# Strassen products on eight cores: an old layer's last M6 and M7 go between M2 and M1 of the new layer, token sums follow need, W3's blocks load on another queue

## What is computed

```python
xn = _layernorm(x)                      # x: 8192 x 2048, float32
xz = einsum('bsh,ih->bsi', xn, W_in)    # 2048 -> 2 x 4096
x1, z = split(xz, 2)
x1 = einsum('bsk,ik->bsi', x1, conv_w)  # 4096 -> 4096
a = einsum('bsi,hi->bsh', (x1 * D) * silu(z), W_out)    # 4096 -> 2048
h = relu(xn @ W1.T + b1); h = relu(h @ W2.T + b2)       # 2048 -> 4096 -> 4096
out = x + a + (h @ W3.T + b3)                           # 4096 -> 2048
```

## Time and profile before

| | us |
|---|---|
| median of 3 runs | 1953.33 |
| lowest, highest | 1846.08, 2122.7 |
| the profiled execution | 1847.9 |
| its span on the slowest core (core 5) | 1846.4 |
| spans of the eight cores | 1838.6 to 1846.4 |

### The profile page before, as it was taken

One profiled execution on the slowest core, in us unless ns is written; L12 is line 12 of the kernel. 1 busy time (PEld: TensorE's weight loads), 2 busy tenths in 40 slices (PEclk: granted clock), 3 DMA queues, 4 the chain that ended last, 5 costly groups with the idle time before them and its releaser, 6 DMA issues.

```text
span 1846.4 us, 24801 instructions; the slowest of 8 cores (1838.6 to 1846.4 us)
## 1 busy us (share of the span) xinstructions
PE 1770.9 (96%) x9984; PEld 978.1 (53%) x9984; DVE 902.7 (49%) x1134; ACT 223.7 (12%) x350; POOL 214.3 (12%) x269
## 2 busy tenths in 40 slices
PE   2799999999999999999999999999999899999998
PEld 2344444444444444444444344444444788888887
DVE  6644444444444584444444743333332844475443
ACT  2111112222222200000000011111111000000000
POOL 0033320000000000000000000000000022222221
PEclk9899999999999999999999999999999999999999
DMA  9277774444448544444445822233337565785532
GB/s 298 71 237 213 219 218 137 137 131 124 125 134 274 155 125 125 126 123 134 137 137 169 264 88 98 104 110 114 114 114 250 174 204 176 259 272 163 181 116 69
DMA packets 58016, 296.34 MB, mean 161 GB/s; under 512 B 7600, under 2 KB 7600, under 8 KB 40368
## 3 DMA queue, kind: packets, MB, share of 16 engines
q1 hardware_dynamic: 28800, 159.40, 30.2%
q0 software_dynamic: 28816, 135.28, 21.3%
q10 hardware_dynamic: 288, 0.08, 0.0%
HBM read 227.62 MB, written 67.11 MB: 160 GB/s over the span
## 4 chain that ended last, share of the span: by engine, by line
PE 92%; DVE 5%; DMA 2%; issue 1%; ACT 0%; POOL 0%; DVEq 0%; SPq 0%; POOLq 0%; ACTq 0%
PE ps L292 73%; PE ps L748 19%; DVE sF L239 3%; DMA sF<-H2S 1%; DVE sST L311 1%; DMA sF<-X 1%; DVE sM L332 0%; DVE sW L239 0%; PE ps L347 0%; ACT sF L369 0%; DVE sM L813 0%; DVE sM L515 0%; DVEq L72 0%; POOL OUT L789 0%; POOL PS L789 0%
## 5 line engine op out<-in xcount | busy, mean ns | idle before, releaser
L292 PE MATMUL ps<-sF,sW 128*128 128x512 bf16 (+1 forms) x6272 | 1358.9, 379 | 17.1 <-DVE sM L459 9.0
L292 PEld LDWEIGHTS ps<-sF,sW 128*128 128x128 f16 x6272 | 612.9, 98 | 762.9 <-issue 28.3
L239 DVE TENSOR_TENSOR sW<-sW 128x1024 f16<-128x1024 f16 (+1 forms) x480 | 443.3, 954 | 168.2 <-DMA sW<-W 133.1
L748 PE MATMUL ps<-sW,sF 128*128 128x256 f16 x3584 | 397.2, 274 | 14.1 <-DVE sF L239 4.9
L748 PEld LDWEIGHTS ps<-sW,sF 128*128 128x128 bf16 x3584 | 352.1, 98 | 59.5 <-issue 17.0
L459 DVE TENSOR_TENSOR sM<-ps,sM 128x512 f32<-128x512 f32 x80 | 55.3, 691 | 340.7 <-ACT sM L454 340.7
L515 DVE TENSOR_TENSOR sM<-ps,sM 128x512 f32<-128x512 f32 (+1 forms) x160 | 110.2, 689 | 123.8 <-PE ps L292 123.7
L454 ACT ACTIVATE sM<-ps 128x512 f32<-128x512 f32 x80 | 47.8, 597 | 606.3 <-PE ps L292 606.3
L239 DVE TENSOR_TENSOR sF<-sF 128x2048 bf16<-128x2048 bf16 (+1 forms) x90 | 103.2, 1219 | 5.3 <-DMA sF<-H2S 5.3
L496 ACT ACTIVATE sM<-sM,sCN 128x512 bf16<-128x512 f32 x64 | 46.2, 722 | 232.9 <-DVE sM L515 232.8
L464 DVE TENSOR_TENSOR sM<-ps,sM 128x512 f32<-128x512 f32 x80 | 55.0, 687 | 24.1 <-PE ps L292 24.1
(11 more groups left out here) (34 smaller groups left out, 315.5 us busy)
## 6 DMA issues: line engine op xcount, KB each, us to landing
sW<-W SPq DMA_DIRECT2D x48, 1024.0 KB, 8.7
sW<-WC SPq DMA_DIRECT2D x32, 1024.0 KB, 6.8
sW<-WX SPq DMA_DIRECT2D x32, 512.0 KB, 8.0
sW<-WZ SPq DMA_DIRECT2D x32, 512.0 KB, 6.7
sW<-W SPq DMA_DIRECT2D x32, 512.0 KB, 6.8
sW<-WO SPq DMA_DIRECT2D x16, 1024.0 KB, 8.0
sF<-X SPq DMA_DIRECT2D x8, 1024.0 KB, 15.0
X1S<-sM POOLq DMA_DIRECT2D x16, 512.0 KB, 8.0
```

The lines of the kernel that those rows point to most:

```text
L239: return line.do(lambda e: e.tensor_tensor(out, a, b, ALU.subtract if sub else ALU.add), c)
L292: return e.matmul(ps[bank][:], sW[:, c0 + k * 128:c0 + (k + 1) * 128], rhs[:, k * TH:(k + 1) * TH], start=st0, stop=last, skip_group_check ...
L748: return e.matmul(ps[bank][:, lo:lo + CW], lhs[:, k * TH + tp * 128:k * TH + (tp + 1) * 128], w[:, k * CW:(k + 1) * CW], start=start, stop ...
```

## The change

- Into WC and W2 (`first`, the first pair of these layers): `phase_a` issues M6 and M7 of the old layer's last pair between M2 and M1 of the new pair. VectorE's order becomes: weight sums for M5 and M2 of the next pair, d, close 6, form 3, close 7, form 4, e, the weight sum for the next M1, those for M6 and M7, form 6, and, after M3 and M4 are issued and their results sent out, form 7. Into WC, form 3 takes the slot that old M3 and M4 read, and comes ahead of all of it.
- Into WO: the last pair's M6, M7, closes and store (`finish_pairs`) move from ahead of WO's M5 to between its M2 and M1. All three weight sums of the first chunk and form 1 come first, then close 6, form 3, close 7. `e_start` is filled there. Form 4 comes between d and e, form 6 after e, form 7 between the closes of M3 and those of M4. The first four residual loads are issued after `phase_oa`.
- In all chunks the sums for M6 and M7 come after both e; in the first chunk of a layer the sum for M7 comes after the closes of M3.
- Into W3: the four blocks of H2S load on SP's queue, among the weight blocks of the next chunk, on four semaphores of their own. Forms 6 and 7 of W3 move from the end of WO's last chunk into W3's first chunk. 

```diff
--- before.py
+++ after.py
@@ -117,6 +117,7 @@
     c_st = [ctr(f"st{i}") for i in range(3)]
     c_zl = [ctr(f"zl{i}") for i in range(3)]
     c_fl = [ctr(f"fl{i}") for i in range(7)]
+    c_hl = [ctr(f"hl{i}") for i in range(4)]
     c_bx = [ctr(f"bx{i}") for i in range(2)]
     c_bs = [ctr(f"bs{i}") for i in range(2)]
     c_b3 = ctr("b3")
@@ -546,13 +547,14 @@
         LAND = {"22": 5, "11": 2, "12": 6, "21": 7}
         tk_raw = {}
 
-        def load_blk(s, blk, toks):
+        def load_blk(s, blk, toks, q=pool):
             slot = SLOT[s][LAND[blk]]
-            pool.need(*toks)
-            pool.need(*stored[SRC[s]])
+            c = c_fl[slot] if q is pool else c_hl[BLK[blk]]
+            q.need(*toks)
+            q.need(*stored[SRC[s]])
             o = BLK[blk] * 8192
-            tk_raw[(s, blk)] = pool.do(lambda e: e.dma_start(f_at(slot), dram[SRC[s]][:, o:o + 8192]),
-                                       c_fl[slot], 16)
+            tk_raw[(s, blk)] = q.do(lambda e: e.dma_start(f_at(slot), dram[SRC[s]][:, o:o + 8192]),
+                                       c, 16)
 
         def new_forms(s, m, toks=()):
             def at(x):
@@ -571,11 +573,14 @@
             f_sum(s, m, f_at(SLOT[s][m]), at(a), at(b), sub, BF16, 4, 8192, need)
 
 
-        def phase_a(g):
+        def phase_a(g, between=None):
+
             si, _ = pairs[g]
             a, b, c = banks(g)
             product((g, 5), si, 5, a, g, [tk_c22.get(g - 2)])
             product((g, 2), si, 2, b, g, [tk_c11.get(g - 2), tk_s2.get(g - 2)])
+            if between is not None:
+                phase_c(between)
             product((g, 1), si, 1, c, g, [tk_e.get(g - 2)])
             n = FM[si]["nk"] * 128
             for m in (5, 2, 1):
@@ -606,36 +611,49 @@
             st = FM[si]
             kind = st["kind"]
             s_next = si + 1
-
-            phase_a(g)
-            if g > 0:
-                phase_c(g - 1)
-
-            snap_b(g)
-            if g + 1 < NG:
+            first = p == 0 and si >= 3
+
+            if first:
+                phase_a(g, between=g - 1)
+                snap_b(g)
+                if si == 3:
+                    new_forms(si, 3, [tk_pe[(g - 1, 4)]])
                 w_sum(g + 1, 5)
                 w_sum(g + 1, 2)
-            make_d(g)
-            if g + 1 < NG:
+                make_d(g)
+                close(g - 1, 6)
+                if si != 3:
+                    new_forms(si, 3, [tk_pe[(g - 1, 6)]])
+                close(g - 1, 7)
+                new_forms(si, 4, [tk_pe[(g - 1, 7)]])
+                make_e(g)
                 w_sum(g + 1, 1)
-            make_e(g)
-            w_sum(g, 6)
-            w_sum(g, 7)
-            first = p == 0 and si >= 3
-            if g > 0:
-                close(g - 1, 6)
-            if first:
-                new_forms(si, 3, [tk_pe[(g - 1, 6)]])
-            if g > 0:
-                close(g - 1, 7)
-            if first:
-                new_forms(si, 4, [tk_pe[(g - 1, 7)]])
+                w_sum(g, 6)
+                w_sum(g, 7)
                 new_forms(si, 6)
-                new_forms(si, 7)
+            else:
+                phase_a(g)
+                if g > 0:
+                    phase_c(g - 1)
+                snap_b(g)
+                if g + 1 < NG:
+                    w_sum(g + 1, 5)
+                    w_sum(g + 1, 2)
+                make_d(g)
+                if g + 1 < NG:
+                    w_sum(g + 1, 1)
+                make_e(g)
+                w_sum(g, 6)
+                w_sum(g, 7)
+                if g > 0:
+                    close(g - 1, 6)
+                    close(g - 1, 7)
             phase_b(g)
             a, b, _ = banks(g)
             emit_final(g, "12", ps[a][:], tk_pe[(g, 3)])
             emit_final(g, "21", ps[b][:], tk_pe[(g, 4)])
+            if first:
+                new_forms(si, 7)
 
             load_ready(g - 1, 6)
             last = is_last(g)
@@ -711,14 +729,11 @@
                                 ay[:, i * 2048:(i + 1) * 2048], sub))
             wtok[(si, c, m)] = got
 
-        phase_c(L)
-        close(L, 6)
-        close(L, 7)
-        store_pair(L)
         a_l, b_l, c_l = banks(L)
         a_k, b_k, c_k = banks(L - 1)
         OB = {"A": [6, 7], "B": [a_k, b_k], "C": [c_k, c_l]}
         ob_tok = {6: [], 7: [], a_k: [tk_c22[L - 1]], b_k: [tk_c11[L - 1]], c_k: [tk_e[L - 1]], c_l: [tk_e[L]]}
+        e_start = []
 
         def o_product(si, c, m, extra):
             s = 5 + si
@@ -753,9 +768,6 @@
                 tk_pe[("o", si, c, m, u)] = t
             wfree[wslot[(si, c, key)]] = [t]
 
-
-        e_start = [t for g in (L - 1, L) for t in (tk_c22.get(g), tk_c11.get(g), tk_o.get((g, "22")), tk_o.get((g, "11")))]
-
         ot = {}
         items = [(si, c, m, u) for si in range(2) for c in range(NCH) for m in (3, 4, 6, 7) for u in range(2)]
         tk_rl, tk_ro, tk_rst = {}, {}, {}
@@ -828,10 +840,11 @@
         for i in range(9):
             wfree[i] = [t for t in slot_toks(i) if t is not None]
 
-        def o_prepare(si, c, slots):
+        def o_prepare(si, c, slots, then=lambda key: None):
 
             for key, s in zip(("11", "12", "21", "22"), slots[:4]):
                 o_load(si, c, key, s)
+                then(key)
             return slots[4:7]
 
         chunks = [(si, c) for si in range(2) for c in range(NCH)]
@@ -846,64 +859,84 @@
         sum_slots[0] = o_prepare(0, 0, order)
         o_sum(0, 0, 5, sum_slots[0][0])
         new_forms(5, 1, [tk_pe[(L, 1)]])
-
+        o_sum(0, 0, 2, sum_slots[0][1])
+        o_sum(0, 0, 1, sum_slots[0][2])
         PREF = 4
+
+        def finish_pairs():
+
+            phase_c(L)
+            close(L, 6)
+            new_forms(5, 3, [tk_pe[(L, 6)]])
+            close(L, 7)
+            store_pair(L)
+            refresh(late)
+
+            e_start.extend(t for g in (L - 1, L) for t in (tk_c22[g], tk_c11[g], tk_o[(g, "22")], tk_o[(g, "11")]))
 
         def phase_oa(x):
             si, c = chunks[x]
 
             def free_of(which, key):
                 return lambda u: ob_tok[OB[which][u]] if x == 0 else [ot[(key, u)]]
-            ex5, ex2, ex1 = free_of("A", "c22"), free_of("B", "c11"), free_of("C", "e")
-            o_product(si, c, 5, ex5)
+            o_product(si, c, 5, free_of("A", "c22"))
+            o_product(si, c, 2, free_of("B", "c11"))
             if x == 0:
-                o_sum(si, c, 2, sum_slots[x][1])
-            o_product(si, c, 2, ex2)
-            if x == 0:
-                o_sum(si, c, 1, sum_slots[x][2])
-            o_product(si, c, 1, ex1)
+                finish_pairs()
+            o_product(si, c, 1, free_of("C", "e"))
+
+        def close_items(x, which):
+            for i in which:
+                n = 8 * x + i
+                o_close(n)
+                r_store(n)
+                if n + PREF < len(items):
+                    r_load(n + PREF)
 
         for x, (si, c) in enumerate(chunks):
             s = 5 + si
             n0 = 8 * x
+            phase_oa(x)
             if x == 0:
                 for n in range(PREF):
                     r_load(n)
-            phase_oa(x)
             for u in range(2):
                 o_snap(si, c, u)
                 o_d(si, c, u)
-            o_sum(si, c, 6)
+            if x == 0:
+                new_forms(5, 4, [tk_pe[(L, 7)]])
             for u in range(2):
                 o_e(si, c, u)
-            o_sum(si, c, 7)
-            if x == 0:
-                new_forms(5, 3, [tk_pe[(L, 6)]])
-                new_forms(5, 4, [tk_pe[(L, 7)]])
-                new_forms(5, 6)
-                new_forms(5, 7)
+            if c == 0:
+                new_forms(s, 6)
+            o_sum(si, c, 6)
             o_product(si, c, 3, lambda u: [ot[("d", u)]])
             o_product(si, c, 4, lambda u: [ot[("s2", u)]])
             nxt = x + 1 < len(chunks)
+            switch = c == NCH - 1 and si == 0
             if nxt:
 
                 mine = [wslot[(si, c, k)] for k in (5, 2, 1, "11", "22")]
                 if x == 0:
                     spare = late
                 slots = spare + mine
-                sum_slots[x + 1] = o_prepare(*chunks[x + 1], slots)
-            switch = c == NCH - 1 and si == 0
+                after = {}
+                if switch:
+                    after = {"12": ("22", 5), "21": ("11", 2)}
+                sum_slots[x + 1] = o_prepare(*chunks[x + 1], slots, lambda key: [
+                    load_blk(6, blk, [tk_pe[("o", si, c, m, 1)]], sp) for blk, m in [after[key]]] if key in after else None)
+                if switch:
+                    load_blk(6, "12", [tk_pe[("o", si, c, 3, 1)]], sp)
+                    load_blk(6, "21", [tk_pe[("o", si, c, 4, 1)]], sp)
+            if c == 0:
+                close_items(x, (0, 1))
+                o_sum(si, c, 7)
+                new_forms(s, 7)
+                close_items(x, (2, 3))
+            else:
+                o_sum(si, c, 7)
```

(29 more changed lines are left out.)

## The result

The changed kernel took 1829.88 us (median of four, 1827.66 to 2153.15), its profiled execution 1831.39; the kernel before, in the same four rounds, 1899.7 (1846.01 to 2122.7). The ratio is 0.9908 (95% interval 0.988 to 0.9937).

The account below looks back on a forecast made before the run. TensorE bounds the kernel: a floor of 1818.5 us plus 0.8 left at W2 and 1.5 at WO gives a span of 1820.8, with 1.5 around it 1822 us, 1.4% under the profiled 1847.9; 80% range 1816 to 1836.

Parts of the forecast that it names:

- The measure and the floor: Whole kernel: TensorE bounds it; core 5 loses 29.2 us at four layer changes; without such losses the floor is 1818.5.
- snap distances: Time between ScalarE copies that follow each M2, less the products between: what each layer change costs.
- Into WC: Change of layer into WC: nothing waits any more, all 4.2 us lost there come back.
- Into W2: Change of layer into W2: gain 4.2 of 5.0 us, about 0.8 left, VectorE standing behind late weights.
- Into WO: Change of layer into WO: of 12.2 us lost 10.7 gained, 1.5 left for late residuals.
- 1445.5 + 9.7 + 0.7 + 5.8: At WO: last pair's store leaves, lands, residual load issues and lands; tile in at 1461.7, in effect 0.4 late.
- the prediction's own price: At WO, in the late-residuals rival: a stretch at the lower clock behind a stop costs 1.7 us.
- Into W3: Change of layer into W3: blocks issued earlier on SP's queue, nothing waits, all 7.8 us come back.
- The price of 5.8: Median landing time of residual loads, 5.8 us, used in the chain at WO.
- WO's residuals come late: Rival at WO: store again takes 17.8, loads 5.8; 9.8 us on top, 1832; chance 16%.
- The one on SP's queue: Rival at W3: chunk 4's weights land late behind 2 MB blocks on SP's queue, kernel slower, 1903; chance 4%.
- the prediction's own signs of being wrong: VectorE waiting on WO's residual, a wait on sF at W2 over 2, VectorE waiting for weights in W3.

Follow-up runs that it names:

- e9_best: Changed kernel with W3's blocks on GpSimd's queue at their old places and WO's first residual loads freed from the last store; lowest 1820.57 us, ratio 0.9818.
- e10_hold: As e9_best, with the weights of W2's third pair held until block 21 has landed; 1820.04 to 1820.46 us, ratio 0.9811.
- e11_peold: Changed kernel with TensorE's order as before everywhere, VectorE's as changed; no time given, on cores 4 to 7 WC 20.72, W2 27.17 or 27.18, WO 83.56.
- e6_w3pool: Changed kernel with W3's four blocks back on GpSimd's queue at their old places, new order of sums kept; lowest 1822.6 us, ratio 0.9901.
- e7_tiny: Changed kernel with W3's blocks 12 and 21 cut to 128 of 8192 columns, on SP's queue; 1824.62 us in one execution.
- e8_woold: Changed kernel with old M6 and M7, closes and store back ahead of WO's M5, order of sums as changed; 1825.85 us in one execution.

## Why the prediction was right or wrong

- *The measure and the floor.* Right. TensorE is the bound, and the losses by snap distances were what there was to gain: 29.2 on core 5. On core 0 the forecast took core 5's for three of the four; by its own snaps it lost 27.4 against the 27.2 taken. With nothing or next to nothing of them left, cores 0 and 2 end at 1818.7 and 1818.2; forecast 1818.5. The cores of e9_best and e10_hold at full clock end at 1815.6 to 1819.2. 29.2 us are 1.6% of the span, so no core could become 2% faster by losing its stops, and none did.
- *Into WC.* Right: 20.72 on every core. But the gain was put beside the move of M6 and M7; e11_peold shows that it is the order of the sums.
- *Into W2.* About right in size: 0.8 was left by forecast, 0 to 1.8 by measurement (2.3 on one core of e6_w3pool). In cause only in part: the forecast had VectorE wait for the weights alone. On core 6 it waits 1.35 for them, and 0.49 and 1.17 for the blocks of forms 3 and 4, for which the forecast had no wait.
- *Into WO.* The chain store, load, close and its length were right: 1445.5 + 9.7 + 0.7 + 5.8 was the sum, 16.2 from the store's issue to the tile; core 6 has 12.0 + 0.7 + 3.9 = 16.6, the store 2.3 over its price, the load 1.9 under it. The mis-sized term is what followed. I took 1.5 for TensorE; it stood 0.53 + 2.08 = 2.6 and then had a stretch from 1465 with a granted clock of 0.66, which I had kept for the rival. At 1.7 by the prediction's own price that makes 4.3 of core 6's 4.6. The four loads are also issued 0.7 apart and took 3.9 to 5.7, so the second close waited another 1.13. And the step before was wrong in kind: I let the gain of 12.2 hang on the move, without asking what the sums' new places alone would do.
- *Into W3.* Here the prediction failed. It looked after one neighbour of the blocks on SP's queue, the weights, and found 16.7 us to spare, rightly: the last of them landed 16.0 after its issue at 1586.4. For the other neighbour it wrote that "POOL's stores and residual loads lose a hold". They lost a queue's wait and got the blocks beside them: 12.6 to 20.2 us instead of 3.5 to 6.7, and the 0 that was forecast to be left at W3 became up to 5.4. The price of 5.8 that was in the text for such a load was not used here, nor a load's need for bandwidth at all. It also took form 3's late block as the cause to cure, when the same change had just moved form 3 behind the closes that it held up.
- *The number.* 1822 against 1827.66 to 1831.39, inside the range of 1816 to 1836. 26 us of gain forecast from the profiled execution, 16.5 measured from it, two thirds. Of the 9.4 us between, 5.4 are W3's, 3.1 WO's, 0.6 W2's on core 6.
- *The rivals.* None came as told. "WO's residuals come late" is nearest: store 12.0 rather than 17.8. The one on SP's queue looked at the weights behind the blocks and not at GpSimd's loads beside them. Of the prediction's own signs of being wrong one came, VectorE's wait for the residual at WO (2.66 on core 6). At W3 it had named a wait for weights; what came was the wait for residual tiles.

The page "DMA: Bandwidth & Descriptors" of the Trainium skill (section on queues, rings and completion order) has DMA engines take turns between queues by packets. The runs bear that out in direction: residual loads ahead of the blocks in the same queue took 3.5 to 6.7 us, and with the blocks on another queue they took three to four times as long. The same page of the Trainium skill (section on the anatomy of one DMA, SWDGE path) has 2.0 us plus bytes at 436 GB/s, which makes an estimate of 2.6 for such a load. The traces are above it: 3.4 to 4.8 in e6_w3pool and e7_tiny, up to 20.2 in the changed kernel.

## What to carry to other kernels

When a large transfer is moved to another queue so that it starts earlier, list every small transfer that will then run beside it and price the one that a compute engine waits for; a queue that makes the large one wait protects the small ones ahead of it, and not those behind it, so it matters which of them are urgent. When an edit changes the order of products and the order of the sums behind them, predict and test them apart: here most of the gain is in VectorE's order (by e6_w3pool, e8_woold and e11_peold all that was lost at WC, WO and W3, 24.3 us on core 5), and the move of the products is worth 0.7 to 3.0 us at one of its three places. Look behind each stop of TensorE for a stretch of lower clock: stops of 2.0 and 2.1 us here had one behind them, worth 1.5 to 1.7 us more, though not every stop has.

## What the runs showed of the hardware

- A residual tile of 256 KB took 4.2 to 4.8 us while the core moved 182 GB/s (DMA share 0.63), and 12.6 to 20.2 beside 2 MB blocks at 298 GB/s (0.96), though the blocks were on another queue. Behind such blocks in the same queue a 256 KB load took 20.5 to 23.6.
- TensorE's stops of 2.08 us at WO, before (core 5) and after (core 6), and of 2.02 us at W3 were followed by five microseconds with a mean granted clock of 0.66, 0.66 and 0.70. In the kernel before, on core 5, the clock stayed at 1.00 behind the stops of 1.44 and 1.57 us at W2 and behind one of 2.56 us at W3 (1664.67), so the length of the stop alone does not tell it.
- Whether a stop appears differs from core to core in one execution: W3's distance is 97.81 on core 0 and 103.20 on core 6 with the same program, since the landings differ (from 1601.0 on, core 0's slow tile took 16.9, core 6's from 1602.2 took 20.2) and the first 6 us or so of VectorE's waiting between 1595 and 1660 reach no product: 5.9 us of it on core 0 cost nothing, 6.5 on core 1 cost 0.3, 9.3 on core 3 cost 2.9.
- On one chip the profiled executions had mean granted clocks of 0.935 to 0.962, and VectorE's waits no longer reached TensorE: its waits at WO and W3 were 0.3 at most where they had been up to 4.4. A kernel's stops can't be judged there.
